# A Transformer layer with gated experts on one core: the outer products move from VectorE to GpSimd

## The reference, cut to what matters

```
vs = v * src_comp[..., None]
kv = jnp.cumsum(jnp.einsum('bhld,bhlm->bhldm', k, vs), axis=2)
x  = jnp.einsum('bhld,bhldm->bhlm', qs, kv) * sink_alloc[..., None]
attn = x @ Wo + bo
```

## Time and profile before

| | |
|---|---|
| median of 3 runs | 476.23 us (474.59 to 477.46) |
| the profiled execution | 476.75 us, of it 475.0 us from the first to the last instruction (the span) |
| VectorE busy | 396.8 us, 84% of the span |
| TensorE (matmul) busy | 383.2 us, 81% |
| GpSimd busy | 216.2 us, 46% |
| ScalarE busy | 172.6 us, 36% |
| mean granted TensorE clock | 0.887 of full speed |

### The profile page before, as it was taken

The page is one execution under the profiler, slowest core; times in us unless marked ns, Lnnn a source line. Parts: engine busy times, 40 slices in busy tenths (PEclk is TensorE's granted clock), DMA queues, the critical chain, the costliest instruction groups (busy, mean ns, idle before and its releaser), DMA issues.

```text
span 475.0 us, 6561 instructions
## 1 busy us (share of the span) xinstructions
PE 383.2 (81%) x2020; PEld 280.0 (59%) x2020; DVE 396.8 (84%) x939; ACT 172.6 (36%) x279; POOL 216.2 (46%) x199
## 2 busy tenths in 40 slices
PE   5656785679898988889888998699888896899792
PEld 1545564467648773677457664696457663863642
DVE  3439968999699999999999987999999999885522
ACT  2221071135332562417441552227441551164231
POOL 1015524843385257722773356623773258454101
PEclk9556977697897999989999899698998999999898
DMA  8116006200440018000710054000810053000000
GB/s 280 47 34 166 1 0 148 74 1 1 89 134 0 2 27 217 1 1 0 188 58 2 1 116 130 1 0 0 203 40 0 1 127 72 2 0 22 1 22 23
DMA packets 19854, 26.51 MB, mean 56 GB/s; under 512 B 1648, under 2 KB 9968, under 8 KB 19824
## 3 DMA queue, kind: packets, MB, share of 16 engines
q1 hardware_dynamic: 19680, 25.95, 20.7%
q10 hardware_dynamic: 144, 0.21, 0.2%
HBM read 7.29 MB, written 2.10 MB: 20 GB/s over the span
## 4 chain that ended last, share of the span: by engine, by line
DVE 43%; PE 25%; issue 20%; POOL 7%; ACT 2%; DMA 2%; DVEq 1%; POOLq 0%; ACTq 0%
DVE kv L849 7%; DVE cum_kv L855 7%; PE pB L333 4%; PE pO L384 4%; DVE stats L860 4%; PE pY L473 4%; POOL prod L664 3%; DVE n L879 3%; POOL rstd L657 2%; DMA vb<-vs 2%; DVE res L983 2%; DVE x L879 2%; DVE mv L864 1%; DVE gel L975 1%; DVE cum_q L745 1%
## 5 line engine op out<-in xcount | busy, mean ns | idle before, releaser
L664 POOL TENSOR_TENSOR prod<-cum_kv,q_fac 128x512 f32<-128x512 f32 x64 | 92.6, 1451 | 46.5 <-DVE cum_kv L855 41.8
L384 PE MATMUL pO<-s_wor,prod 128*128 128x128 f32 x512 | 77.3, 304 | 23.0 <-POOL prod L664 22.9
L384 PEld LDWEIGHTS pO<-s_wor,prod 128*128 128x128 f32 x512 | 71.0, 214 | 40.5 <-POOL prod L664 33.9
L655 POOL TENSOR_TENSOR var_eps<-mv,s_con 128x4 f32<-128x4 f32 x32 | 9.2, 287 | 102.3 <-DVE mv L864 102.3
L849 DVE TENSOR_TENSOR kv<-k,vb 128x512 f32<-128x512 f32 x64 | 47.4, 741 | 5.6 <-issue 3.0
L855 DVE TENSOR_TENSOR_SCAN cum_kv<-p_ones,cum_kv,kv 128x512 f32<-128x512 f32 x32 | 40.4, 1273 | 0.9
L621 ACT ACTIVATE relu<-pG,s_att 128x512 f32<-128x512 f32 x32 | 21.9, 686 | 52.6 <-PE pG L455 52.5
L855 DVE TENSOR_TENSOR_SCAN cum_kv<-p_ones,kv 128x512 f32<-128x512 f32 x32 | 38.5, 1212 | 1.0
L454 PE MATMUL pG<-x2T,s_moe 128*128 128x512 f32 x64 | 34.4, 619 | 4.2 <-DVE gel L975 4.2
L473 PEld LDWEIGHTS pY<-s_moe,gel 128*128 128x128 f32 x256 | 34.8, 215 | 3.4 <-issue 3.4
L707 POOL TENSOR_TENSOR e_norm<-esrc,s_con 128x64 f32<-128x64 f32 x8 | 2.9, 358 | 72.7 <-ACT esrc L572 72.7
(11 more groups left out here) (129 smaller groups left out, 754.4 us busy)
## 6 DMA issues: line engine op xcount, KB each, us to landing
vb<-vs SPq DMA_DIRECT2D x64, 256.0 KB, 4.4
xT<-x_t SPq DMA_DIRECT2D x8, 256.0 KB, 4.4
xt<-x SPq DMA_DIRECT2D x8, 256.0 KB, 4.8
out<-y SPq DMA_DIRECT2D x8, 256.0 KB, 2.3
s_moe<-moe_w SPq DMA_DIRECT2D x1, 836.0 KB, 10.1
s_wor<-wo_rep SPq DMA_DIRECT2D x1, 512.0 KB, 7.9
s_ffn<-ffn_w SPq DMA_DIRECT2D x1, 512.0 KB, 8.5
s_con<-consts SPq DMA_DIRECT2D x1, 500.0 KB, 4.7
```

Source lines behind the costliest of these rows:

```text
L384: mm = pe.matmul(pO3[:, s, :], prod[:, m % 4, s * P:(s + 1) * P], s_wor[:, m, :], start=(m == 0 and s == 0), stop=(m == DH - 1), skip_grou ...
L664: pool.tensor_tensor(prod[:, m % 4, :], cum_kv[t.par][:, m, :], q_fac[t.par][:, :], ALU.mult).then_inc(prod_ready, 1)
```

## The change

GpSimd makes the outer products, and VectorE's list is reordered. On GpSimd outer products 4 to 7 stand between products 1 to 4 at the front of the step, 0 ahead of `inverse_std(b, 1)`, 1 and 2 ahead of product 0, and 3 behind `scaled_n2(b)`. VectorE's scans 5, 6 and 7 of tile b are spread between the scans of q and k, the two `second_relu(d)` and `k_times_cum_q` of the next tile. The instructions, their sizes and buffers stay the same.

```diff
@@ GpSimd
+            def outer_product(t, m):
+                if m == 0:
+                    pool.wait_ge(k_ready, t.n + 1)
+                pool.wait_ge(vb_loaded[m], 16 * (t.n + 1))
+                wait(pool, cumkv_ready, DH * t.n + m - 2)
+                pool.tensor_tensor(kv[:, m % 3, :], k[t.par][:, :], vb[:, m, :], ALU.mult).then_inc(kv_ready, 1)
...
                 if C: outer_residual(c)
-                if B: product(b, 1); product(b, 2)
+                if B: outer_product(b, 4); product(b, 1)
                 if C: inverse_std(c, 2)
-                if B: product(b, 3); product(b, 4); product(b, 5); product(b, 6); product(b, 7); inverse_std(b, 0)
+                if B: outer_product(b, 5); product(b, 2); outer_product(b, 6); product(b, 3)
+                if B: outer_product(b, 7); product(b, 4); product(b, 5); product(b, 6); product(b, 7); inverse_std(b, 0)
...
                 if C: constant_residual(c)
+                if A: outer_product(a, 0)
                 if B: inverse_std(b, 1)
-                if A: product(a, 0)
+                if A: outer_product(a, 1); outer_product(a, 2); product(a, 0)
                 if B: scaled_n2(b)
+                if A: outer_product(a, 3)
@@ VectorE
-            def outer_product(t, m):
-                dve.wait_ge(vb_loaded[m], 16 * (t.n + 1))
-                wait(dve, cumkv_ready, DH * t.n + m - 2)
-                dve.tensor_tensor(kv[:, m % 3, :], k[t.par][:, :], vb[:, m, :], ALU.mult).then_inc(kv_ready, 1)
...
-                if B: outer_product(b, 4); cumulate_kv(b, 3); cumulate_kv(b, 4); outer_product(b, 5)
+                if B: cumulate_kv(b, 3); cumulate_kv(b, 4)
                 if C: normalise(c, 2)
-                if B: cumulate_kv(b, 5); outer_product(b, 6); cumulate_kv(b, 6); outer_product(b, 7)
+                if A: cumulate_q(a)
+                if B: cumulate_kv(b, 5)
+                if A: cumulate_k(a)
+                if D: second_relu(d, 2)
+                if B: cumulate_kv(b, 6)
+                if D: second_relu(d, 3)
+                if A: k_times_cum_q(a, 0)
                 if B: cumulate_kv(b, 7)
-                if A: cumulate_q(a); cumulate_k(a)
-                if D: second_relu(d, 2); second_relu(d, 3)
-                if A: k_times_cum_q(a, 0)
...
-                if A: query_factor(a); outer_product(a, 0); cumulate_kv(a, 0)
+                if A: query_factor(a); cumulate_kv(a, 0)
                 if B: normalise(b, 1)
-                if A: outer_product(a, 1)
                 if C: second_relu(c, 0); second_relu(c, 1)
-                if A: outer_product(a, 2); cumulate_kv(a, 1); outer_product(a, 3); cumulate_kv(a, 2)
+                if A: cumulate_kv(a, 1); cumulate_kv(a, 2)
```

## The result

| | before | after |
|---|---|---|
| median | 476.85 us (474.59 to 478.05, 4 runs) | 513.75 us (511.89 to 515.57, 4 runs) |
| the profiled execution's span | 475.0 us | 513.8 us |
| mean granted TensorE clock | 0.887 | 0.856 |

The ratio is 1.078, with a 95% interval of 1.072 to 1.084: slower by 37 us. The prediction was 514.

The account below looks back on a forecast made before the run. VectorE was taken as the bound before the change. Six steps of 5.5 us (+33), step 0 (+1), the last tile's terms (+3.5) and a partly hidden stall (-1) gave 476.75 + 37 = 514 us, range 484 to 530.

Parts of the forecast that it names:

- the walk of one step: One full step, from `vs` to the next `vs` in three stretches, was to grow by 5.5 us.
- the end: Stretch from `vs` to `moments(b, 2)`: +1.4 us against 14.34.
- the front: Stretch from `moments(b, 2)` to `attention_residual`: +3.4 us against 16.98.
- the part behind it: From `attention_residual` on: +0.7 us, as `expert_out` and two `head_sums` must precede `inverse_denominators`.
- the collision: GpSimd operations without gaps each hold one VectorE instruction; `normalise(c, 2)` takes 5.0 us plus 0.2, against 2.1 today.
- What VectorE gives up: 64 outer products of 741 ns: 47.4 us in the whole run, 5.9 us in a step.
- GpSimd's row: GpSimd's list of operations in a step puts `attention_residual` no earlier than 31.4 us behind `vs`; today 31.3.
- The price of 1.24 us: Time assumed for one outer product on GpSimd, taken from `product`, the same operation and size.
- a cover: The 3.6 us between product 7's end and `attention_residual`, filled by next-tile q and k work; the reordering spends it.
- GpSimd's row alone: Rival: `normalise` stays at 2.1 us and a step grows by 1.3: 488 us, range 480 to 500, chance 0.25.
- The clock: Rival: pauses bring TensorE's lower clock into each step, 3.5 us more: up to 535 us, chance 0.10.
- The signs: Expected in the profile: `moments(b, 2)` and `attention_residual` wait, `normalise(c, 2)` about 5 us, GpSimd busy some 300, step 56.

Follow-up runs that it names:

- experiment 8: Changed kernel with scans 5 to 7 of tile b together and `normalise(c, 2)` reading one operand from PSUM, its factor `rstd` left out: 477.32 us, ratio 1.005.
- experiment 1: Changed kernel, outer products still on GpSimd, with VectorE's scans 5 to 7 of tile b put together again behind `normalise(c, 2)`: 475.44 us, ratio 1.0005.
- experiment 6: Changed kernel with the four instructions of `normalise(c, 2)` reading one operand from PSUM, its factor `rstd` left out: 503.5 us, ratio 1.061.
- experiment 3: Changed kernel with unread TensorE products of 256 columns, two ahead of `reduce_out` 6 and four ahead of 7: 495.61 us, ratio 1.047.
- experiment 5: Changed kernel with only the scans of q and k ahead of scans 6 and 7; `second_relu` and `k_times_cum_q` behind them: 480.66 us, ratio 1.016.
- experiment 2: Kernel before, outer products still on VectorE, with its scans 5 to 7 spread as in the changed kernel: 520.85 us, ratio 1.0975.
- experiment 9: Kernel before with `normalise(c, 2)` made by ScalarE, VectorE keeping one small instruction for the bias: 473.54 us, ratio 0.998.

## Why the prediction was right or wrong

The time was right to 0.3 us, and so close a hit was luck. In the walk of one step the end came out 1.1 us too large, the front 0.5 and the part behind it 0.8 too small (5.5 forecast, 5.7 measured in tile 4), and the weight went to the collision where the order of the scans has it.

**What VectorE gives up is eaten by GpSimd's row: right.** The row gave 31.4 us from `vs` to `attention_residual`; with the scans together it measured 31.5 and 31.0. Experiment 8 shows the row as a bound: with the collision gone nothing is won. In experiment 1 VectorE comes to `attention_residual` 1.1 us behind the row, so that the two bounds lie close there. The match of the total flatters the sum: the first copy lands 4.0 us behind `vs` and not 5.2, and with 4.0 the sum is 30.2. In experiment 1 `reduce_out(7)` ended 30.4 us behind `vs` (226.89 to 257.29). The price of 1.24 us held: outer products follow each other at 1.22 to 1.23 us and last 1.27. By contrast the Trainium skill (GPSIMD Engine Reference, Elementwise — side-by-side cycle accounting) has 4497 ns for 2048 elements, from which I estimate 1.12; the traces here have no `product` and no outer product under 1.25. (The one operation of that size with two inputs that is shorter, 1.04 us, takes one of them from four repeated columns and runs once.) The upper bound, 1.45, was the collisions: with the outer products gone from VectorE, `product` fell to 1.33. I had put GpSimd at some 300 us and it is 275.6. The new operations at my price (64 x 1.24 = 79) on top of 216.2 make 296, with nothing taken off for the collisions that vanish: `product` lost 7.9 us, `outer_residual` 3.8, `scaled_n2` 3.2 and the first half of `inverse_std` 2.7.

**The collision: right in size, wrong in weight.** Four held instructions, 5.0 us: measured 4.96. The rule of the Trainium skill (SBUF — State Buffer, Who interferes with whom) that I had weighed against the change is borne out, and the measured price is a whole GpSimd operation for each instruction held: the 32 instructions of `normalise(c, 2)`, four at a tile, take 1170 ns on average, those of the last tile (1.12 us for four) included. But I let it carry the front. Experiment 1 has it whole, experiment 8 removes it from the same order, and both take 475 to 477 us; experiment 6 removes it from the kernel after and keeps 29 of the 37 us. In the first order GpSimd's row takes as long anyway, in the second the wait for `k` takes its place.

**The step that failed: the spreading had no price of its own.** My walk of the front counted five scans, two `second_relu` and `k_times_cum_q` ahead of product 7, in one sum with the collision. It came to M+20.4 (measured 20.92), since such a sum is indifferent to which of its terms is at fault. Of the order I only said that it spends a cover. I never asked what the sum would be with the terms of the next tile behind scan 7: M+9.0, three scans to M+12.5, product 7 by GpSimd's row at M+15, as experiment 1 has it. So before experiment 1 I still expected 494 from it, and it gave 475.

**GpSimd's row alone, 488 us: its condition was wrong.** I tied this rival to a cheap collision. The order decides it, not the collision: with the collision whole and the scans together the kernel takes 475 us. (Its sum was off as well: 3.8 + 9 x 1.24 + 1.3 is 16.3, not 16.4, so the front loses 0.7 and the rival comes to about 486.)

**The clock: a rival at 0.10 and in fact two fifths to a half of the loss.** I gave it only what would come on top of 514, up to 535. It is 15 to 18 us by experiment 3, inside the 514. The term that was mis-sized is "behind it, +0.7": measured +1.5 in tile 4, and in the tiles 2, 5 and 6 `inverse_denominators` waits 2.75 to 2.85 us for `pB`. There `expert_out` takes 1.9 us and each `head_sums` 1.7 to 1.9, against 1.06 and 1.04 at the full clock; in tile 4 the clock is back for `head_sums` (1.02 and 1.04). Two other terms were too large. One is the end of the step, +1.4 (measured +0.3: the first copy landed 4.0 us behind `vs` and not 5.2, and of `normalise(b, 1)` only one instruction was held here, for GpSimd itself waited for a copy). The other is the front, +3.4, taken as bare lateness: of the measured +3.9 I estimate 1.35 for `reduce_out(7)` at the lower clock and for the last product (0.9 and 0.45, as in experiment 5), which leaves 2.6.

**The sum over steps.** From tile 0 to tile 6 the kernel after needs 338.7 us from one `attention_residual` to the last, before 306.5: 5.4 us a step against 5.5 forecast. They are uneven, from 1.8 to 9.8. The smallest belongs to the step in which the kernel before has its stall of 2.96 us (294.80); the rest was not followed.

**The signs.** `moments(b, 2)` waits for `outer_residual`, `normalise` takes 5 us, a step takes 56.6 us: these three came out. `attention_residual` waits for `pO`, but for 2.8 us a step and not 1 to 2, and GpSimd is busy for 276 us and not 300. All would have looked alike had the collision been the cause. They test the walk, not its terms.

## What to carry to other kernels

When a change moves work ahead of a link of the chain that ends last, price the move by itself: read how long the link's result lies unused today (here 2.5 us), and what exceeds that is what costs, in every step; here 2.4 us inside it cost 7 us over the whole run and 2.5 more beyond it 29. Here two fifths to a half of the loss came on top through the clock, since TensorE began to pause. Moving work to an engine with idle time gains nothing if its new operations all stand in the one row that the chain runs through; sum that row first. A forecast that meets the time is no proof of its reasons: one run with a single part undone told more here than all the signs that had come true.

## What the runs showed of the hardware that was not expected

Behind pauses of 0.81, 1.29 and 1.70 us between groups of eight matmuls TensorE's granted clock was 0.50, in a stretch that had been at 1.00 before. Filling the last two with 6 unread products of 256 columns brought the ratio from 1.078 to 1.047. The length of a pause alone does not tell: in experiment 2 TensorE waited 2.40 us and `reduce_out(6)` still took 1.16 us, and only behind a second pause of 2.32 did `reduce_out(7)` take 2.08, while in experiment 9 a single pause of 2.62 was enough.

```profile
278.44 1.16 PE L384 MATMUL pO<-s_wor,prod 128*128 128x128 f32 x8 [2.40 <-POOL prod L664]
281.92 2.08 PE L384 MATMUL pO<-s_wor,prod 128*128 128x128 f32 x8 [2.32 <-POOL prod L664]
```

When GpSimd's operations follow without a gap, the holding is one to one: the four instructions of `normalise(c, 2)` took 4.7 to 5.0 us together at seven tiles, and 1.12 at the last one, where GpSimd was idle. The four instructions with one operand in PSUM instead took 1.12 us beside the same row of GpSimd (experiments 6 and 8), as undisturbed ones do. The holding also reaches 128x4 instructions: `shift` of experiment 9 took 1.22 us.
